# Grouped-query attention stage: two of TensorE's output units cut differently around its waits, one VectorE add moved ahead of a reciprocal, and the halves of the output-weight split exchanged between VectorE and GpSimd

## The chip, the cores and the metric

One core of one Trainium2 chip. The metric is device time in microseconds (us) of one execution; the kernel before took 3282.12 us, the median of 3 runs (3276.79 to 3284.53).

## What is computed

A two-layer gated transformer block with 16 x 128 rows of width 1024. Each layer adds a gated cross attention and a gated feed-forward part to the residual. The change lies in the third of these four parts, the grouped-query attention:

```python
q = (query @ Wq).reshape(b, t, h, d)          # h = 32 heads, d = 128
k = (key @ Wk).reshape(b, t, kv_h, d)         # kv_h = 8
v = (value @ Wv).reshape(b, t, kv_h, d)
q = apply_rope(q); k = apply_rope(k)
logits = MAX_ATTN_VAL * jnp.tanh(q.k * ATTN_MULT / MAX_ATTN_VAL)
logits = jnp.where(m, logits, -1e+30)
weights = jax.nn.softmax(logits, axis=-1)
attn = jnp.einsum('bkgtT,bTkd->btkgd', weights, v).reshape(b, t, h * d)
x = x + jnp.tanh(g_xattn[1]) * (attn @ Wo)
```

## The kernel before

The function `gqa_stage` runs 32 steps: 4 groups of 4 batches, and in each group the 8 key/value heads. A step n projects four query heads, rotates them, makes scores and probabilities for the 4 batches, sums and weights the values, normalises, and multiplies by that head's slice of `Wo` into the residual. Every engine has its own program, a list written out by hand, and semaphores tie them together. Each product in single precision is made of three matmuls (a high part times a high part, and the two mixed terms), so every operand is split into a rounded `hi`, made by ScalarE (`round_hi`, L1710), and a rest `lo`, made by GpSimd or VectorE (`subtract_hi`, L1569).

- **TensorE**: `attend(n)` and then `project(n + 1)`. `attend` runs `scores` (L1916, 3 matmuls), `values` (2 matmuls of row sums at L1925, 3 at L1931) and, between them, the output units of the step before: `out(u)` is unit u of 8 (batch u // 2, half u % 2), 12 matmuls at L1949, in four quarters of 3 matmuls, one a query head. `project` is 96 matmuls at L1893, 24 for each of the 4 query heads. That is 224 matmuls of 128x512 in a step.
- `scores(n, 0)` waits for all four rotated heads (`rot_lo`). Unit u waits for the add of unit u - 2, since both use one of two banks; units 0, 2, 4, 6 also wait for `at_lo` of their batch, and the four quarters of unit 0 wait for the four quarters of the split output weight. `values(n, b)` waits for `prob_lo` of b and for the reciprocal of b - 1 (`rsum_done`), since there is one bank for the row sums.
- **VectorE**: `rotate(n, i)` is three instructions (L1810 to L1812) that read a projected head from PSUM; it waits until GpSimd has added the head before (`rot_done`). `mask_probs` (L1844) multiplies by the mask, `normalise` is a reciprocal of 512 columns (L1850) and a product (L1853), `add(u)` is the add of an output unit into the residual (L1830), and `wo_split_dve` makes the `lo` of a quarter of the output weight (L1569).
- **GpSimd**: `rotated(n, i)` adds the two rotated parts (L1650), waits for ScalarE's rounding and subtracts (L1569). After heads 0 and 1 it makes the `lo` of an output-weight quarter (`wo_split`). Earlier in the step it makes the `lo` of the probabilities, of the attention output (`at`) and of the four quarters of the next `Wq` slice (`wq_split`); in the last step of a group these four stand behind the `lo` of the new activations.
- **ScalarE**: tanh and exp of the scores, the rounding of everything, in the order of `body_act`; the four quarters of the output weight are rounded one after the other, right behind rotated head 0.

In the last step the output weight lies in the buffer of `Wq` (`wo_last`), and the 8 output units run behind the last `values`, with the next stage's work between them.

Of the kernel before, what the change touches and what calls it, by code (L numbers as in the profile page):

```python
# [30 lines left out]
FIRST = 1  # L31
# [1416 lines left out]
def gqa_stage(nc, banks, kept_tiles, x_in, xnT, k_in, v_in, gate, Wq, Wo, x_out):  # L1448
# [8 lines left out]
    G = NH // NKV  # L1457
# [10 lines left out]
    def sem(name):  # L1468
        return nc.alloc_semaphore(name="g_" + name)
# [3 lines left out]
    def split(n, shape):  # L1473
        lo, hi = sb(n + "_lo", shape, F32R), sb(n + "_hi", shape, F32R)
        return {"lo": lo, "hi": hi, "raw": sb(n + "_raw", shape, over=n + "_lo")}
# [8 lines left out]
    wo, at = split("wo", [P, G, DM]), split("at", [P, G, BANK])  # L1484
# [3 lines left out]
    wo_last = {t: wq[t][:, :, :].rearrange("p (h a) n -> p h (a n)", h=G) for t in ("raw", "hi", "lo")}  # L1488
# [10 lines left out]
    wo_lo, wo_lo_dve, xn_lo, wq_lo = sem("wo_lo"), sem("wo_lo_dve"), sem("xn_lo"), sem("wq_lo")  # L1499
# [52 lines left out]
    def part(name, i, piece):  # L1552

        if name == "xn":
            c = (2 * i + piece) * SEQ
            return lambda t: t[:, :, c:c + SEQ]
        n = (KT if name == "wq" else G) // 4
        m = (2 * i + piece) * n
        return lambda t: t[:, m:m + n, :]

    def bcols(b):
        return slice(b * SEQ, (b + 1) * SEQ)

    def heads(t):
        return t.rearrange("p (h t) -> p h t", h=G)

    def subtract_hi(engine, buf, view):

        return engine.tensor_tensor(view(buf["lo"]), view(buf["raw"]), view(buf["hi"]).bitcast(F32), ALU.subtract)  # L1569

    sp, pool, act, dve, pe = nc.sync, nc.gpsimd, nc.scalar, nc.vector, nc.tensor
# [61 lines left out]
    def xn_split(g, i):  # L1633
        for m in range(2):
            pool.wait_ge(xn_hi, FIRST + g * 4 + 2 * i + m + 1)
            subtract_hi(nc.gpsimd, xn, part("xn", i, m)).then_inc(xn_lo, 1)

    def wq_split(n, m):
        pool.wait_ge(wq_hi, FIRST + n * 4 + m + 1)
        subtract_hi(nc.gpsimd, wq, part("wq", m // 2, m % 2)).then_inc(wq_lo, 1)  # L1640

    def wo_split(n, m, buf):
        pool.wait_ge(wo_hi, FIRST + n * 4 + m + 1)
        subtract_hi(nc.gpsimd, buf, part("wo", m // 2, m % 2)).then_inc(wo_lo, 1)

    def rotated(n, i):

        pool.wait_ge(rot_mul, FIRST + n * NR + i + 1)
        dst = q["raw"][:, i, :]
        nc.gpsimd.tensor_tensor(dst, dst, rot_b[:, :], ALU.add).then_inc(rot_done, 1)  # L1650
        pool.wait_ge(rot_hi, FIRST + n * NR + i + 1)
        subtract_hi(nc.gpsimd, q, lambda t: t[:, i, :]).then_inc(rot_lo, 1)
# [12 lines left out]
    def body_pool(z):  # L1665
        n = z.n

        def prob_split(b):
            pool.wait_ge(prob_hi, FIRST + n * NB + b + 1)
            subtract_hi(nc.gpsimd, prob[b % 2], lambda t: t[:, :]).then_inc(prob_lo, 1)  # L1670

        def attn_split(b):
            pool.wait_ge(at_hi, FIRST + n * NB + b + 1)
            subtract_hi(nc.gpsimd, at, lambda t: t[:, :, bcols(b)]).then_inc(at_lo, 1)

        early = not z.last and not z.group_end
        prob_split(0)
        prob_split(1)
        attn_split(0)
        prob_split(2)  # L1680
        if early:
            wq_split(n + 1, 0)
            wq_split(n + 1, 1)
        if z.group_end:
            xn_split(z.g + 1, 0)
        attn_split(1)
        prob_split(3)
        if z.group_end:
            xn_split(z.g + 1, 1)
        if early:  # L1690
            wq_split(n + 1, 2)
            wq_split(n + 1, 3)
        attn_split(2)
        if z.group_end:
            for m in range(4):
                wq_split(n + 1, m)
        if z.last:
            for m in range(2):
                wo_split(n, m, wo_last)
        attn_split(3)  # L1700
        if not z.last:
            for i in range(NR):
                rotated(n + 1, i)
                if i < 2:
                    wo_split(n, i, wo)


    A = nc.scalar.activation
# [79 lines left out]
    def wo_split_dve(n, m, buf):  # L1788
        dve.wait_ge(wo_hi, FIRST + n * 4 + m + 1)
        subtract_hi(V, buf, part("wo", m // 2, m % 2)).then_inc(wo_lo_dve, 1)  # L1790
# [42 lines left out]
    def body_dve(z):  # L1833
        n = z.n

        def add(*units):
            if not z.first:
                for u in units:
                    add_output(n - 1, u)

        def mask_probs(b):
            e = prob[b % 2]["raw"][:, :]
            dve.wait_ge(exp_done, FIRST + n * NB + b + 1)
            V.tensor_tensor(heads(e), heads(e), keep[:, :].rearrange("p (o t) -> p o t", o=1)  # L1844
                            .to_broadcast([P, G, SEQ]), ALU.mult).then_inc(masked, 1)

        def normalise(b):
            dve.wait_ge(sum_done, FIRST + n * NB + b + 1)
            dve.wait_ge(attn_done, FIRST + n * NB + b)
            V.reciprocal(rsum[:, :], p_sum[:, :]).then_inc(rsum_done, 1)  # L1850
            dve.wait_ge(rsum_done, FIRST + n * NB + b + 1)
            dve.wait_ge(pv_done, FIRST + n * NB + b + 1)
            V.tensor_tensor(at["raw"][:, :, bcols(b)], heads(p_pv[b % 2][:, :]), heads(rsum[:, :]), ALU.mult)\  # L1853
                .then_inc(attn_done, 1)

        if not z.first:

            dve.wait_ge(res_in, 64 * z.res_group + 64)
        add(0)
        mask_probs(0)  # L1860
        add(1)
        mask_probs(1)
        add(2)
        normalise(0)
        mask_probs(2)
        add(3)
        normalise(1)
        add(4)
        mask_probs(3)
        add(5)  # L1870
        normalise(2)
        if z.last:
            wo_split_dve(n, 2, wo_last)
        add(6, 7)
        normalise(3)
        if z.last:
            wo_split_dve(n, 3, wo_last)
        if not z.last:
            for i in range(NR):
                rotate(n + 1, i)  # L1880
                if 1 <= i < 3:
                    wo_split_dve(n, i + 1, wo)


    M, T = nc.tensor.matmul, nc.tensor.transpose
# [22 lines left out]
    def scores(n, b):  # L1908
        if b == 0:

            pe.wait_ge(rot_lo, FIRST + (n + 1) * NR)
            pe.wait_ge(k_land, 16 * n + 16)

        pe.wait_ge(tanh_done, FIRST + n * NB + max(b - 1, 0))
        for t, (p, r) in enumerate(SPLIT):
            mm = M(heads(p_s[b % 2][:, :]), k[p][:, bcols(b)], q[r][:, :, bcols(b)],  # L1916
                   start=(t == 0), stop=(t == 2))
        mm.then_inc(s_done, 1)
# [15 lines left out]
    def output(n, u, w, heads_=range(G)):  # L1934

        b, half_ = u // 2, u % 2
        if heads_[0] == 0:
            if half_ == 0:
                pe.wait_ge(at_lo, FIRST + n * NB + b + 1)

            pe.wait_ge(y_added, FIRST + n * NU + max(u - 1, 0))
        for h in heads_:
            if u == 0:
                if h < 2:
                    pe.wait_ge(wo_lo, FIRST + n * 2 + h + 1)
                else:
                    pe.wait_ge(wo_lo_dve, FIRST + n * 2 + h - 1)
            for t, (p, r) in enumerate(SPLIT):
                mm = M(p_y[u % 2][:, :], at[p][:, h, bcols(b)], w[r][:, h, half_ * BANK:(half_ + 1) * BANK],  # L1949
                       start=(h == 0 and t == 0), stop=(h == G - 1 and t == 2))  # L1950
        if heads_[-1] == G - 1:
            mm.then_inc(y_done, 1)

    def attend(n, first=False):
        def out(u, heads_=range(G)):
            if not first:
                output(n - 1, u, wo, heads_)

        out(0)
        out(1)  # L1960
        scores(n, 0)
        scores(n, 1)
        out(2)
        scores(n, 2)
        values(n, 0)
        out(3)
        out(4, range(0, 2))
        scores(n, 3)
        values(n, 1)
        out(4, range(2, G))  # L1970
        out(5)
        out(6, range(0, 1))
        values(n, 2)
        out(6, range(1, G))
        out(7)
        values(n, 3)

# [706 lines left out]
```

## Time and profile before

| | us |
|---|---|
| median of 3 runs | 3282.12 |
| lowest, highest | 3276.79, 3284.53 |
| the profiled execution's own time | 3288.88 |
| its span, from first to last instruction | 3287.1 |

Over the span TensorE's matmuls are busy 94%, VectorE 64%, GpSimd 56%, ScalarE 38%. The grouped-query stage takes from about 1280 us to 3063 us of the span, more than half of it. Engine shares are averages over stages with different limits; what bounds a step is read from the order of time inside one step, which repeats almost unchanged.

### The profile page before, as it was taken

The numbers are of one execution on the slowest core, as the hardware profiler recorded it, in microseconds if no ns is written. First come the engines' busy times: TensorE is split into PE (matmuls) and PEld (weight loads), VectorE is DVE, ScalarE is ACT, GpSimd is POOL, SyncE is SP. The second block draws the span as 40 slices with busy tenths as digits, with TensorE's granted clock in tenths as the row PEclk, the third lists the DMA queues.
The fourth block names the chain that finished last, engine by engine and source line by source line (L and its number), as shares of the span: only waits on it lengthen the run. The fifth ranks groups of instructions, "written<-read, shape, count | busy, mean of one in ns | idle before, by whom it ended". The sixth has DMA issues, their size and how long they took to land. (4 is left out here: it accounts for less than half of the span.)

```text
span 3287.1 us, 41110 instructions
## 1 busy us (share of the span) xinstructions
PE 3080.6 (94%) x14547; PEld 2474.0 (75%) x14547; DVE 2093.1 (64%) x2607; ACT 1234.8 (38%) x1898; POOL 1851.3 (56%) x1244
## 2 busy tenths in 40 slices
PE   7999679999999996899999999999999999998799
PEld 6888558788787775677777777777778787777577
DVE  3332357777777753767666767767777677676575
ACT  3111155555555541333333433433333434333222
POOL 4232354454454443667676767676767776764343
PEclk9999889999999997999999999999999999999799
DMA  7343501101111113222233222332222332323221
GB/s 200 107 131 109 180 26 39 65 33 65 53 45 65 52 54 114 102 90 102 89 128 141 102 95 96 121 147 96 96 96 101 129 134 96 111 90 134 84 71 52
DMA packets 171260, 315.53 MB, mean 96 GB/s; under 512 B 10328, under 2 KB 86488, under 8 KB 171144
## 3 DMA queue, kind: packets, MB, share of 16 engines
q1 hardware_dynamic: 171144, 314.04, 27.3%
q8 instruction: 66, 1.08, 0.1%
q14 instruction: 50, 0.41, 0.0%
HBM read 246.90 MB, written 67.11 MB: 96 GB/s over the span
## 5 line engine op out<-in xcount | busy, mean ns | idle before, releaser
L1850 DVE RECIPROCAL g_rsum<-pair 128x512 f32<-128x512 f32 x128 | 429.0, 3351 | 57.1 <-PE pair L1925 57.1
L1893 PE MATMUL pair<-g_xn_hi,g_wq_hi 128*128 128x512 f32 x1024 | 403.9, 394 | 19.1 <-POOL g_wq_lo L1569 14.0
L1893 PE MATMUL pair<-g_xn_lo,g_wq_hi 128*128 128x512 f32 x1024 | 402.5, 393 | 0.0
L1893 PE MATMUL pair<-g_xn_hi,g_wq_lo 128*128 128x512 f32 x1024 | 402.2, 393 | 0.0
L1949 PE MATMUL pair<-g_wo_hi,g_at_hi 128*128 128x512 f32 x992 | 389.6, 393 | 2.4 <-DVE g_res L1830 0.2
L1949 PE MATMUL pair<-g_wo_lo,g_at_hi 128*128 128x512 f32 x992 | 386.2, 389 | 0.0
L1949 PE MATMUL pair<-g_wo_hi,g_at_lo 128*128 128x512 f32 x992 | 386.1, 389 | 0.0
L1569 POOL TENSOR_TENSOR g_wq_lo<-g_wq_raw,g_wq_hi 128x1024 fp32r<-128x1024 f32 x130 | 310.9, 2415 | 0.0
L1569 POOL TENSOR_TENSOR g_at_lo<-g_at_raw,g_at_hi 128x512 fp32r<-128x512 f32 x128 | 180.1, 1407 | 217.6 <-ACT g_at_hi L1710 217.6
L1710 ACT ACTIVATE g_q_hi<-g_q_raw 128x512 fp32r<-128x512 f32 x128 | 81.0, 633 | 535.6 <-POOL g_q_raw L1650 535.6
L1810 DVE TENSOR_TENSOR g_q_raw<-pair,t_cos_q 128x512 f32<-128x512 f32 x128 | 88.5, 692 | 296.2 <-PE pair L1893 256.5
L1650 POOL TENSOR_TENSOR g_q_raw<-g_q_raw,g_rot_b 128x512 f32<-128x512 f32 x128 | 226.0, 1765 | 86.0 <-DVE g_rot_b L1812 86.0
L669 POOL TENSOR_TENSOR a_qs<-a_qs,a_qrec 128x512 f32<-128x512 f32 x128 | 133.9, 1048 | 201.2 <-DVE a_qrec L915 200.3
L1569 POOL TENSOR_TENSOR g_prob_lo<-g_prob_raw,g_prob_hi 128x512 fp32r<-128x512 f32 x128 | 166.6, 1311 | 138.1 <-ACT g_prob_hi L1710 138.1
L1893 PEld LDWEIGHTS pair<-g_xn_hi,g_wq_hi 128*128 128x128 f32 x1024 | 195.0, 190 | 62.9 <-POOL g_wq_lo L1569 16.7
L1844 DVE TENSOR_TENSOR g_prob_raw<-g_prob_raw,t_keep 128x512 f32<-128x512 f32 x128 | 132.5, 1035 | 166.7 <-ACT g_prob_raw L1741 166.7
L1949 PEld LDWEIGHTS pair<-g_wo_hi,g_at_hi 128*128 128x128 f32 x992 | 186.1, 188 | 53.4 <-DVE g_res L1830 14.9
L1893 PEld LDWEIGHTS pair<-g_xn_lo,g_wq_hi 128*128 128x128 f32 x1024 | 195.1, 191 | 40.7
L1893 PEld LDWEIGHTS pair<-g_xn_hi,g_wq_lo 128*128 128x128 f32 x1024 | 194.6, 190 | 40.9
L1569 POOL TENSOR_TENSOR g_q_lo<-g_q_raw,g_q_hi 128x512 fp32r<-128x512 f32 x128 | 165.0, 1289 | 95.1 <-ACT g_q_hi L1710 95.1
L1949 PEld LDWEIGHTS pair<-g_wo_hi,g_at_lo 128*128 128x128 f32 x992 | 186.2, 188 | 39.1
L1949 PEld LDWEIGHTS pair<-g_wo_lo,g_at_hi 128*128 128x128 f32 x992 | 186.3, 188 | 37.9
(251 smaller groups left out, 7333.3 us busy)
## 6 DMA issues: line engine op xcount, KB each, us to landing
g_wq_raw<-in_L_Wq SPq DMA_DIRECT2D x64, 1024.0 KB, 7.3
g_wo_raw<-in_L_Wo SPq DMA_DIRECT2D x62, 1024.0 KB, 6.3
values_split<-c_v SPq DMA_DIRECT2D x64, 256.0 KB, 2.8
keys_split<-c_k SPq DMA_DIRECT2D x32, 512.0 KB, 2.7
g_k<-keys_split SPq DMA_DIRECT2D x32, 512.0 KB, 3.2
g_v<-values_split SPq DMA_DIRECT2D x32, 512.0 KB, 7.7
c_cx_raw<-in_ctxT SPq DMA_DIRECT2D x16, 512.0 KB, 7.4
a_x<-in_x SPq DMA_DIRECT2D x16, 512.0 KB, 4.5
```

The costliest lines, as they stand in the source:

```text
L669: TT(t, t, spread(qrec[r % 2][:, :], DH), ALU.mult).then_inc(qnorm, 1)
L1569: return engine.tensor_tensor(view(buf["lo"]), view(buf["raw"]), view(buf["hi"]).bitcast(F32), ALU.subtract)
L1650: nc.gpsimd.tensor_tensor(dst, dst, rot_b[:, :], ALU.add).then_inc(rot_done, 1)
L1710: return A(view(buf["hi"]), view(buf["raw"]), ACT.Copy)
L1810: V.tensor_tensor(by_batch(a), by_batch(src[:, :]), w(cos, 0, P), ALU.mult)
L1844: V.tensor_tensor(heads(e), heads(e), keep[:, :].rearrange("p (o t) -> p o t", o=1) .to_broadcast([P, G, SEQ]), ALU.mult).then_inc(masked, 1)
L1850: V.reciprocal(rsum[:, :], p_sum[:, :]).then_inc(rsum_done, 1)
L1893: mm = M(bank[:, :], w[a][:, i, cols], x[b][:, i, :], start=(i == 0 and t == 0), stop=(i == KT - 1 and t == 2))
L1949: mm = M(p_y[u % 2][:, :], at[p][:, h, bcols(b)], w[r][:, h, half_ * BANK:(half_ + 1) * BANK], start=(h == 0 and t == 0), stop=(h == G - 1 ...
```

## The change

Three edits in `gqa_stage`, with the same instructions in all; only their order on an engine, and who splits which quarter, differ.

1. TensorE (`attend`): the first quarter of unit 2 goes ahead of the two first scores, the first half of unit 3 ahead of `scores(2)`, the second half of unit 4 ahead of `scores(3)`, the second quarter of unit 6 ahead of `values(2)`.
2. VectorE (`body_dve`): `add(4)` moves from behind the second `normalise` to ahead of it, right behind `add(3)`.
3. Output weight: VectorE now splits quarters 0 and 1, behind its rotations 0 and 1 (before: 2 and 3, behind 1 and 2), and GpSimd quarters 2 and 3, behind its rotated heads 0 and 1 as before (before: 0 and 1). The semaphores that unit 0 waits for are exchanged to match.

```diff
@@ body_pool
         if z.last:
-            for m in range(2):
+            for m in range(2, 4):
                 wo_split(n, m, wo_last)
         attn_split(3)
         if not z.last:
             for i in range(NR):
                 rotated(n + 1, i)
                 if i < 2:
-                    wo_split(n, i, wo)
+                    wo_split(n, i + 2, wo)
@@ body_dve
         mask_probs(2)
-        add(3)
+        add(3, 4)
         normalise(1)
-        add(4)
         mask_probs(3)
         add(5)
         normalise(2)
         if z.last:
-            wo_split_dve(n, 2, wo_last)
+            wo_split_dve(n, 0, wo_last)
         add(6, 7)
         normalise(3)
         if z.last:
-            wo_split_dve(n, 3, wo_last)
+            wo_split_dve(n, 1, wo_last)
         if not z.last:
             for i in range(NR):
                 rotate(n + 1, i)
-                if 1 <= i < 3:
-                    wo_split_dve(n, i + 1, wo)
+                if i < 2:
+                    wo_split_dve(n, i, wo)
@@ output
                 if h < 2:
-                    pe.wait_ge(wo_lo, FIRST + n * 2 + h + 1)
+                    pe.wait_ge(wo_lo_dve, FIRST + n * 2 + h + 1)
                 else:
-                    pe.wait_ge(wo_lo_dve, FIRST + n * 2 + h - 1)
+                    pe.wait_ge(wo_lo, FIRST + n * 2 + h - 1)
@@ attend
         out(1)
+        out(2, range(0, 1))
         scores(n, 0)
         scores(n, 1)
-        out(2)
+        out(2, range(1, G))
+        out(3, range(0, 2))
         scores(n, 2)
         values(n, 0)
-        out(3)
-        out(4, range(0, 2))
+        out(3, range(2, G))
+        out(4)
         scores(n, 3)
         values(n, 1)
-        out(4, range(2, G))
         out(5)
-        out(6, range(0, 1))
+        out(6, range(0, 2))
         values(n, 2)
-        out(6, range(1, G))
+        out(6, range(2, G))
         out(7)
         values(n, 3)
```

How the instructions stand on VectorE behind the rotations of one step, as a piece of the difference (- before, + changed): L1810 to L1812 are one rotation, L1569 is the split of an output-weight quarter.

```order
 L1811 TENSOR_TENSOR g_rot_b<-pair,t_sin_q 64x512
 L1812 TENSOR_TENSOR g_rot_b<-pair,t_sin_q 64x512
-L1810 TENSOR_TENSOR g_q_raw<-pair,t_cos_q 128x512
-L1811 TENSOR_TENSOR g_rot_b<-pair,t_sin_q 64x512
-L1812 TENSOR_TENSOR g_rot_b<-pair,t_sin_q 64x512
 L1569 TENSOR_TENSOR g_wo_lo<-g_wo_raw,g_wo_hi 128x1024
 L1810 TENSOR_TENSOR g_q_raw<-pair,t_cos_q 128x512
```

The first of the two splits now stands behind rotation 0, and rotation 1 behind the split; the second stands behind rotation 1, and between rotations 2 and 3 there is none.

VectorE from the second-to-last mask to the third reciprocal, in the kernel before:

```order
L1844 TENSOR_TENSOR g_prob_raw<-g_prob_raw,t_keep 128x512
L1830 SCALAR_TENSOR_TENSOR g_res<-pair,g_tg,g_res 128x512
L1850 RECIPROCAL g_rsum<-pair 128x512
L1853 TENSOR_TENSOR g_at_raw<-pair,g_rsum 128x4x128
L1830 SCALAR_TENSOR_TENSOR g_res<-pair,g_tg,g_res 128x512
L1844 TENSOR_TENSOR g_prob_raw<-g_prob_raw,t_keep 128x512
L1830 SCALAR_TENSOR_TENSOR g_res<-pair,g_tg,g_res 128x512
L1850 RECIPROCAL g_rsum<-pair 128x512
```

and in the changed one:

```order
L1844 TENSOR_TENSOR g_prob_raw<-g_prob_raw,t_keep 128x512
L1830 SCALAR_TENSOR_TENSOR g_res<-pair,g_tg,g_res 128x512 x2
L1850 RECIPROCAL g_rsum<-pair 128x512
L1853 TENSOR_TENSOR g_at_raw<-pair,g_rsum 128x4x128
L1844 TENSOR_TENSOR g_prob_raw<-g_prob_raw,t_keep 128x512
L1830 SCALAR_TENSOR_TENSOR g_res<-pair,g_tg,g_res 128x512
L1850 RECIPROCAL g_rsum<-pair 128x512
```

The add of unit 4 joins that of unit 3, and the last mask (the second L1844) follows the second product (L1853) directly.

## Rows read from the trace of the kernel before

**Rows 1.** Windows, an ordinary and a group's last step: start:end length, busy per engine, PEclk, DMA, GB/s.

```profile
1549.10:1602.38 53.28, 51.68 (x225) 41.81 (x224) 37.97 (x35) 19.86 (x28) 37.02 (x23) 1.00 0.27 98
1655.66:1713.69 58.03, 51.87 (x226) 41.62 (x224) 42.03 (x37) 24.15 (x33) 41.95 (x26) 0.99 0.47 155
```

**Rows 2.** Timeline, TensorE, one ordinary step: start us, us, instruction, [idle before <-releaser].

```profile
1517.60 0.39 PE L1949 MATMUL pair<-g_wo_hi,g_at_hi 128*128 128x512 f32 x1
...
1524.29 0.49 PE L1916 MATMUL pair<-g_q_hi,g_k 128*128 128x512 f32 x1 [1.09 <-POOL g_q_lo L1569]
...
1529.80 0.50 PE L1925 MATMUL pair<-g_prob_hi,g_ones_r 128*128 128x512 f32 x1 [0.47 <-POOL g_prob_lo L1569]
...
1535.83 0.39 PE L1925 MATMUL pair<-g_prob_hi,g_ones_r 128*128 128x512 f32 x1
...
1541.28 0.50 PE L1949 MATMUL pair<-g_wo_hi,g_at_hi 128*128 128x512 f32 x1
...
1547.99 0.39 PE L1925 MATMUL pair<-g_prob_hi,g_ones_r 128*128 128x512 f32 x1
...
1549.12 0.39 PE L1893 MATMUL pair<-g_xn_hi,g_wq_hi 128*128 128x512 f32 x1
```

**Rows 3.** Timeline, VectorE, rotations 1 to 3 of the same step.

```profile
1506.92 0.69 DVE L1810 TENSOR_TENSOR g_q_raw<-pair,t_cos_q 128x512 f32<-128x512 f32 x1 [3.19 <-PE pair L1893]
...
1509.04 1.54 DVE L1569 TENSOR_TENSOR g_wo_lo<-g_wo_raw,g_wo_hi 128x1024 fp32r<-128x1024 f32 x1
...
1514.48 2.73 DVE L1569 TENSOR_TENSOR g_wo_lo<-g_wo_raw,g_wo_hi 128x1024 fp32r<-128x1024 f32 x1
1518.59 0.69 DVE L1810 TENSOR_TENSOR g_q_raw<-pair,t_cos_q 128x512 f32<-128x512 f32 x1 [1.38 <-POOL g_q_raw L1650]
```

**Rows 4.** Timeline, ScalarE's four output-weight roundings and GpSimd, the same stretch.

```profile
1505.66 3.89 ACT L1710 ACTIVATE g_wo_hi<-g_wo_raw 128x1024 fp32r<-128x1024 f32 x4
...
1507.10 2.41 POOL L1569 TENSOR_TENSOR g_wo_lo<-g_wo_raw,g_wo_hi 128x1024 fp32r<-128x1024 f32 x1
1509.46 2.27 POOL L1650 TENSOR_TENSOR g_q_raw<-g_q_raw,g_rot_b 128x512 f32<-128x512 f32 x1
...
1513.73 2.41 POOL L1569 TENSOR_TENSOR g_wo_lo<-g_wo_raw,g_wo_hi 128x1024 fp32r<-128x1024 f32 x1
1516.07 2.29 POOL L1650 TENSOR_TENSOR g_q_raw<-g_q_raw,g_rot_b 128x512 f32<-128x512 f32 x1
...
1520.77 1.29 POOL L1650 TENSOR_TENSOR g_q_raw<-g_q_raw,g_rot_b 128x512 f32<-128x512 f32 x1 [0.37 <-DVE g_rot_b L1812]
```

**Rows 5.** Timeline, VectorE, from the second add to the third reciprocal.

```profile
1527.27 0.74 DVE L1830 SCALAR_TENSOR_TENSOR g_res<-pair,g_tg,g_res 128x512 f32<-128x512 f32 x1
...
1530.66 3.36 DVE L1850 RECIPROCAL g_rsum<-pair 128x512 f32<-128x512 f32 x1 [1.21 <-PE pair L1925]
...
1534.66 0.68 DVE L1844 TENSOR_TENSOR g_prob_raw<-g_prob_raw,t_keep 128x512 f32<-128x512 f32 x1
1535.26 0.74 DVE L1830 SCALAR_TENSOR_TENSOR g_res<-pair,g_tg,g_res 128x512 f32<-128x512 f32 x1
1536.48 3.36 DVE L1850 RECIPROCAL g_rsum<-pair 128x512 f32<-128x512 f32 x1 [0.48 <-PE pair L1925]
...
1540.48 0.74 DVE L1830 SCALAR_TENSOR_TENSOR g_res<-pair,g_tg,g_res 128x512 f32<-128x512 f32 x1
1541.14 2.16 DVE L1844 TENSOR_TENSOR g_prob_raw<-g_prob_raw,t_keep 128x512 f32<-128x512 f32 x1
...
1543.88 3.34 DVE L1850 RECIPROCAL g_rsum<-pair 128x512 f32<-128x512 f32 x1
```

**Rows 6.** Timeline, GpSimd, the first two quarters of the next query weight.

```profile
1537.99 4.76 POOL L1569 TENSOR_TENSOR g_wq_lo<-g_wq_raw,g_wq_hi 128x1024 fp32r<-128x1024 f32 x2
```

**Rows 7.** Timeline, TensorE, first projection behind the last step of a group.

```profile
1713.69 0.79 PE L1893 MATMUL pair<-g_xn_hi,g_wq_hi 128*128 128x512 f32 x1 [4.61 <-POOL g_wq_lo L1569]
```

**Rows 8.** Timeline, TensorE, fourth quarter of unit 0 behind the last step.

```profile
3018.11 0.50 PE L1949 MATMUL pair<-g_wq_hi,g_at_hi 128*128 128x512 f32 x1 [1.35 <-DVE g_wq_lo L1569]
```

## Prediction

> **What bounds the kernel now.** First the windows of the grouped-query stage: an ordinary step takes 53.28 us, the last step of a group 58.03 us [rows 1]. Then TensorE's timeline through one ordinary step. Five matmuls without a wait take 1549.12 - 1547.99 = 1.13 us, so 0.227 us each, and the 224 of a step 50.8 us. TensorE is the bound, and only 53.28 - 50.8 = 2.4 to 2.5 us a step are waits. There are three [rows 2], and the first matmuls behind each run about 0.1 us late:
> - ahead of the first scores: units 0 and 1 (24 matmuls, 5.45) run from 1517.60 to 1523.05, the scores start at 1524.29, so 1.24. They wait for the last rotated head.
> - ahead of the first values (1529.80): of the 5.51 us since the scores' start, 21 matmuls and the late start take 4.87, so 0.64; GpSimd's `prob_lo` was late.
> - ahead of unit 6 (1541.28): 23 matmuls (5.22) since 1535.83, so 0.23 at its bank, which the add of unit 4 frees at 1540.48 + 0.74 = 1541.22 [rows 5].
>
> Two more views show what these waits hang on. VectorE's and GpSimd's timelines of the rotations: VectorE's split of a quarter, asked for at 1509.04, ends at 1510.58, which is 1.07 behind the end of GpSimd's split (1509.51); GpSimd's add, begun at 1509.46, ends at 1511.73, 1.15 behind VectorE's. The second pair (1514.48 and 1516.07) ends 1.07 behind 1516.14 and 1.15 behind 1517.21 in the same way, where an unhindered add takes 1.29 [rows 3, 4]. So these two engines exclude each other here, instruction by instruction. The mask at 1541.14 (2.16 instead of 0.68) ends at 1543.30, 0.55 behind the end (1542.75) of the second query-weight quarter [rows 5, 6]. The rotations and the reciprocals read PSUM and keep their lengths.
>
> **The change, edit by edit.** No instruction is added or taken away, and no DMA moves, so everything is a shift of waits.
>
> *Exchange of the output-weight quarters.* ScalarE's four roundings run 1505.66 to 1509.55, about 0.95 apart [rows 4]. GpSimd's first split took quarter 0, ready early, and began at 1507.10. It now needs quarter 2, ready at about 1508.60, begins at 1508.68 and ends at 1511.09. VectorE splits quarter 0 from 1507.14 (GpSimd's subtraction ends there) to about 1508.2, so rotation 1 slips from 1506.92 to 1508.1 and ends at 1510.2 (2.12 long [rows 3]). It asks for quarter 1 at 1510.1, waits for GpSimd, and ends at 1511.09 + 1.07 = 1512.16. GpSimd's add of head 1 then ends at 1512.16 + 1.15 = 1513.31, where it was 1511.73. Its second split comes 2.00 later as before (1511.73 to 1513.73 [rows 4]), 1515.31 to 1517.72. Now the gain: no VectorE split stands there, so the add of head 2 takes 1.29 and ends at 1517.65 + 1.29 = 1518.94, against 1518.36. Rotation 3 waits for exactly this add [rows 3], and the scores for rotation 3. So the first scores start 0.58 later: **+0.58 us**. Bounds: 0 if the add of head 2 is not held at all, and 0.58 + 1.0 if one more collision of the kind in rows 3 and 4 falls in. I take 0.58, since each link has its row.
>
> *First quarter of unit 2 ahead of the scores.* 27 matmuls end at 1517.60 + 6.13 = 1523.73, before the scores can start (1524.87). It costs nothing and fills 0.68 of that wait.
>
> *From the first scores to the last values*, counted from the scores' start as 0. Before, the last values started at 1547.99 - 1524.29 = 23.70. Now:
> - scores 0 and 1 and three quarters of unit 2 end at 1.46 + 2.04 = 3.50. Unit 3 needs the add of unit 1, which ends at 1527.27 + 0.74, so 3.72 [rows 5]: a new wait until 3.78. Six matmuls and a late start: 5.25. Scores 2: 5.93.
> - the first values start at 5.93 without a wait (`prob_lo` is there at 5.51). The second come 26 matmuls later, 11.83. The first reciprocal starts 0.65 behind the values (1535.83 to 1536.48 [rows 2, 5]), at 6.58; before it was 6.37.
> - VectorE: mask 4.00 behind the reciprocal, then 0.60 (mask) and twice 0.66 (adds): second reciprocal at 12.50, its sums at 12.48. The moved add just fills the idle 0.48 [rows 5]. The last mask is asked for 4.00 later, at 16.50.
> - GpSimd's second query-weight quarter starts 9.71 behind the first reciprocal (1540.37 - 1530.66 [rows 5, 6]) and ends 12.09 behind it: 16.29 to 18.67. The mask is late by 0.21 and waits for all of it: end at 18.67 + 0.55 = 19.22. The add of unit 5 ends at 19.88, the third reciprocal runs 19.80 to 23.14; before it started at 19.59.
> - TensorE reaches unit 7 at 11.83 + 34 x 0.227 = 19.55 and waits for that add until 19.94, then has 12 matmuls, and meets the last values at 22.77. These wait for the third reciprocal: 23.20, and with the late start the next projection begins at 24.43. Before: 24.83.
>
> So the two old waits (0.64 and 0.23, with their late starts) are gone and three others come, because VectorE's third reciprocal does not come earlier. **-0.40 us.**
>
> The length of a mask that waits is taken from the row: 0.55 behind GpSimd's end [rows 5, 6]. The Trainium skill, "SBUF — State Buffer", section "Who interferes with whom", says that the second instruction blocks fully until the first has finished. Read strictly that puts the whole 0.68 behind, and VectorE's chain 0.13 later; the sum would be +0.31 a step and 3293 us. The row decides for 0.55, since it shows this very pair.
>
> A bound of the -0.40 below: -1.43, the next section's first rival; above, +0.2, if VectorE's whole chain is 0.6 later.
>
> *Sum.* An ordinary step gains +0.58 - 0.40 = +0.18 us. There are 31 intervals between first projections; the first has no output units, 3 end a group. 27 x 0.18 = 4.9 us. In a group's last step the projection waits 4.76 us for GpSimd, whose chain through the probabilities sets it [rows 7]: there only the delays count, 0.58 + 0.21 = 0.8, three times, 2.4 us. In the last step quarter 3 of unit 0 waited for VectorE's split [rows 8]; now quarter 1 does, so 6 more matmuls (1.4 us) stand behind it, but VectorE's first split no longer waits for the third rounding (about 1.9 us, two roundings): I take 0, with 1.5 either way. Sum **+7.3 us**. The profiled execution, 3288.88 us, becomes 3296.2; it lies 6.8 above the median, so the median goes from 3282.12 to **3289.4 us**. About 0.2%, 6.6 us, is what a measurement here can tell from no change.
>
> **The rivals.**
> - *The mask gets ahead* (faster). Everything at that place hangs on 0.21 us: is the last mask asked for before the second query-weight quarter begins, it takes 0.68. The reciprocal can start at 17.8, ends at 21.1, unit 7 and the last values do not wait, the next projection starts at 22.27 + 1.13 = 23.40, so 1.43 earlier than before. With the exchange's 0.58: -0.85 a step, 27 x -0.85 + 2.4 = -21 us, **3262 us**. For it: only 0.21 us decide. Against: all the durations repeat within 0.03 us, and the margin is a difference of chains that start from the same reciprocal. 0.12. The Trainium skill, "SBUF — State Buffer", section "Who interferes with whom", has this as its rule: of a VectorE instruction with two SBUF inputs and a GpSimd one that reads SBUF, whoever issues first gets the shared port pair.
> - *The exchange is free* (faster). If GpSimd's add of head 2 ends no later than before, the -0.40 stays: 27 x -0.40 + 3 x 0.2 = -10 us, **3272 us**. For it: the stall of 1.0 on that add does go. Against: the 1.58 lost at the third rounding is larger. 0.14.
> - *The delay is larger* (slower). A longer idle ahead of the first projection of a group (4.76 grows to 5.4) or one more collision in the rotations: up to 0.3 a step more, +15 us, **3297 us**. It decides if the scores come more than 0.8 late. 0.14.
> - *Nothing moves.* If the new waits just take the place of the old ones and the exchange evens out, 3282 us. 0.06.
>
> **How the numbers follow.** The forecast case has 0.54, and its own range is 3285 to 3294 (0.15 us a step). Of it 0.30 lies above +6.6 us and 0.24 within. With the rivals: faster 0.12 + 0.14 = 0.26; slower 0.30 + 0.14 = 0.44; the same 0.24 + 0.06 = 0.30. The range of 8 in 10 leaves out the first rival and the far end of the third: 3270 to 3299.
>
> **What the changed profile would show.** An ordinary step of 53.4 to 53.5 us. GpSimd's add of head 1 stretched to about 2.3 us and that of head 2 at 1.3. The idle time ahead of the scores still near 1.1 us, now 27 matmuls behind the projection. No wait at the first values; short waits at unit 3, unit 7 and the last values, the last released by the third reciprocal. The last mask about 2.7 us long. A last mask of 0.7 us, or an ordinary step under 53.1, would make the prediction wrong; so would an add of head 2 that ends less than 0.3 later behind the start of the projection.

## Result, and the profile after

| | before, us | changed, us |
|---|---|---|
| median (5 runs each) | 3280.46 | 3297.67 |
| lowest to highest | 3276.79 to 3284.53 | 3293.07 to 3299.62 |
| profiled execution, own time | 3288.88 | 3297.86 |
| its span | 3287.1 | 3296.1 |

The ratio is 1.0049, with a 95% interval of 1.0037 to 1.0060: the change makes the kernel slower by 12 to 20 us. The forecast was +7.3 us (3289.4 us, range 3270 to 3299), with a chance of 0.44 for a slower kernel.

The windows of the changed kernel, as in [rows 1]: first projection of the stage to the last one, from there to the end, one ordinary step, one last step of a group. The columns are those of [rows 1].

```profile
1279.41:2967.61 1688.20, 1607.23 (x6849) 1286.45 (x6849) 1144.69 (x1042) 622.43 (x877) 1135.32 (x690) 0.99 0.30 108
2967.61:3296.10 328.49, 289.84 (x1329) 225.41 (x1327) 201.81 (x306) 92.89 (x168) 132.52 (x96) 0.90 0.23 87
1495.72:1549.41 53.69, 51.92 (x225) 41.74 (x224) 37.36 (x36) 19.85 (x29) 36.03 (x23) 1.00 0.27 98
1656.76:1715.62 58.86, 52.06 (x225) 41.53 (x223) 41.99 (x38) 24.17 (x34) 41.41 (x26) 0.99 0.46 161
```

The same two stretches of the kernel before, first profile:

```profile
1280.67:2955.46 1674.79, 1598.22 (x6848) 1288.74 (x6849) 1162.07 (x1042) 622.31 (x877) 1164.52 (x690) 0.99 0.30 109
2955.46:3287.10 331.64, 292.56 (x1329) 226.64 (x1327) 202.42 (x305) 92.89 (x167) 134.82 (x96) 0.90 0.23 87
```

The loss lies between the first and the last projection: 1688.20 - 1674.79 = 13.4 us. Most ordinary steps are now 53.56 to 53.70 us and were 53.15 to 53.30, so 0.40 more (the first one of a group is some 3 us longer in both kernels, and grows by 0.3 to 0.4); the three last steps of a group are 58.87 to 58.97 and were 57.99 to 58.04, 0.92 more. 27 x 0.40 + 3 x 0.92 = 13.6. VectorE and GpSimd are busy for less time than before (1144.69 and 1135.32 us against 1162.07 and 1164.52), and the stretch is longer all the same.

TensorE's timeline in the ordinary step, which answers to [rows 2]: the scores, unit 3, the first and second values, unit 7, the last values, the next projection.

```profile
1524.79 0.49 PE L1915 MATMUL pair<-g_q_hi,g_k 128*128 128x512 f32 x1 [1.01 <-POOL g_q_lo L1569]
...
1528.57 0.50 PE L1948 MATMUL pair<-g_wo_hi,g_at_hi 128*128 128x512 f32 x1
...
1530.75 0.39 PE L1924 MATMUL pair<-g_prob_hi,g_ones_r 128*128 128x512 f32 x1
...
1536.64 0.39 PE L1924 MATMUL pair<-g_prob_hi,g_ones_r 128*128 128x512 f32 x1
...
1544.84 0.50 PE L1948 MATMUL pair<-g_wo_hi,g_at_hi 128*128 128x512 f32 x1 [0.33 <-DVE g_res L1830]
...
1548.19 0.47 PE L1924 MATMUL pair<-g_prob_hi,g_ones_r 128*128 128x512 f32 x1 [0.34 <-DVE g_rsum L1850]
...
1549.41 0.39 PE L1892 MATMUL pair<-g_xn_hi,g_wq_hi 128*128 128x512 f32 x1
```

The wait at the first values is gone (no bracket at 1530.75; 0.47 before), and in its place stand three: at unit 3 (1528.57, a first matmul of 0.50 instead of 0.39), at unit 7 (1544.84) and at the last values (1548.19), the last two released by an add and by the reciprocal of VectorE. From the scores to the next projection it is 1549.41 - 1524.79 = 24.62 us, where [rows 2] gives 24.83.

GpSimd in the same step, which answers to [rows 4]:

```profile
1508.60 2.41 POOL L1569 TENSOR_TENSOR g_wo_lo<-g_wo_raw,g_wo_hi 128x1024 fp32r<-128x1024 f32 x1 [1.55 <-ACT g_wo_hi L1710]
1510.96 2.27 POOL L1650 TENSOR_TENSOR g_q_raw<-g_q_raw,g_rot_b 128x512 f32<-128x512 f32 x1
...
1515.22 2.39 POOL L1569 TENSOR_TENSOR g_wo_lo<-g_wo_raw,g_wo_hi 128x1024 fp32r<-128x1024 f32 x1
1517.56 1.30 POOL L1650 TENSOR_TENSOR g_q_raw<-g_q_raw,g_rot_b 128x512 f32<-128x512 f32 x1
```

The projection began at 1495.72 here and at 1495.84 in [rows 2]. The first split waits 1.55 us for ScalarE's third rounding, the add of head 1 is stalled (2.27), the add of head 2 is not (1.30). It ends at 1518.86, 23.14 behind the projection's start; before it was 22.52. The scores start 29.07 behind it, before 28.45.

VectorE, which answers to [rows 5]:

```profile
1531.49 3.36 DVE L1850 RECIPROCAL g_rsum<-pair 128x512 f32<-128x512 f32 x1 [1.71 <-PE pair L1924]
1534.88 0.69 DVE L1853 TENSOR_TENSOR g_at_raw<-pair,g_rsum 128x512 f32<-128x512 f32 x1
1535.49 0.68 DVE L1844 TENSOR_TENSOR g_prob_raw<-g_prob_raw,t_keep 128x512 f32<-128x512 f32 x1
1536.09 1.41 DVE L1830 SCALAR_TENSOR_TENSOR g_res<-pair,g_tg,g_res 128x512 f32<-128x512 f32 x2
1537.41 3.35 DVE L1850 RECIPROCAL g_rsum<-pair 128x512 f32<-128x512 f32 x1
1540.79 0.69 DVE L1853 TENSOR_TENSOR g_at_raw<-pair,g_rsum 128x512 f32<-128x512 f32 x1
1541.40 2.72 DVE L1844 TENSOR_TENSOR g_prob_raw<-g_prob_raw,t_keep 128x512 f32<-128x512 f32 x1
1544.04 0.74 DVE L1830 SCALAR_TENSOR_TENSOR g_res<-pair,g_tg,g_res 128x512 f32<-128x512 f32 x1
1544.70 3.34 DVE L1850 RECIPROCAL g_rsum<-pair 128x512 f32<-128x512 f32 x1
```

The moved add has filled the idle 0.48 ahead of the second reciprocal. The last mask is asked for 0.24 us earlier behind the scores than before (16.61 against 16.85) and takes 0.56 longer, 2.72 instead of 2.16, because GpSimd's quarter ends no earlier: 18.78 behind the scores (1543.57), before 18.46. The third reciprocal starts 19.91 behind the scores, before 19.59.

### The profile page after: what moved, and what is told of

Same layout as the page of the kernel before. It is cut to its first block and busy times, and to the rows that moved or that the text cites. A ratio compares the mean times of both kernels' runs of the same rounds, so it can differ in the third digit from the quotient of the medians.

```text
span 3296.1 us, 41110 instructions
## 1 busy us (share of the span) xinstructions
PE 3084.4 (94%) x14547; PEld 2468.6 (75%) x14547; DVE 2076.7 (63%) x2607; ACT 1235.3 (37%) x1898; POOL 1819.9 (55%) x1244
## 5 line engine op out<-in xcount | busy, mean ns | idle before, releaser
L1569 POOL TENSOR_TENSOR g_wq_lo<-g_wq_raw,g_wq_hi 128x1024 fp32r<-128x1024 f32 x130 | 309.5, 2402 | 1.6 <-ACT g_wq_hi L1710 1.6
L1569 POOL TENSOR_TENSOR g_at_lo<-g_at_raw,g_at_hi 128x512 fp32r<-128x512 f32 x128 | 178.9, 1398 | 224.1 <-ACT g_at_hi L1710 224.1
L1844 DVE TENSOR_TENSOR g_prob_raw<-g_prob_raw,t_keep 128x512 f32<-128x512 f32 x128 | 150.1, 1172 | 167.5 <-ACT g_prob_raw L1741 167.5
L1569 POOL TENSOR_TENSOR g_prob_lo<-g_prob_raw,g_prob_hi 128x512 fp32r<-128x512 f32 x128 | 167.1, 1315 | 138.0 <-ACT g_prob_hi L1710 138.0
L1810 DVE TENSOR_TENSOR g_q_raw<-pair,t_cos_q 128x512 f32<-128x512 f32 x128 | 88.6, 692 | 238.2 <-POOL g_q_raw L1650 149.2
L1650 POOL TENSOR_TENSOR g_q_raw<-g_q_raw,g_rot_b 128x512 f32<-128x512 f32 x128 | 195.6, 1528 | 72.0 <-DVE g_rot_b L1812 72.0
L1569 POOL TENSOR_TENSOR g_q_lo<-g_q_raw,g_q_hi 128x512 fp32r<-128x512 f32 x128 | 164.8, 1287 | 95.1 <-ACT g_q_hi L1710 95.1
```

Of the source, the lines that this page charges most:

```text
L1810: V.tensor_tensor(by_batch(a), by_batch(src[:, :]), w(cos, 0, P), ALU.mult)
```

## The experiments

Every kernel was timed beside the kernel before on the same chip (medians of 3280 to 3284 us).

### 1. Without the exchange

The whole change, minus its edits to `body_pool`, `wo_split_dve` and the waits of unit 0:

```diff
-                    wo_split(n, i + 2, wo)
+                    wo_split(n, i, wo)
-                if i < 2:
-                    wo_split_dve(n, i, wo)
+                if 1 <= i < 3:
+                    wo_split_dve(n, i + 1, wo)
```

> The change without its exchange of the output-weight quarters: only TensorE's new unit order and VectorE's moved add. The theory: the exchange alone makes the first scores 0.58 to 0.59 us later, and the rest gives back 0.2 us from the scores to the next projection (24.62 us in the changed kernel against 24.83 before). So an ordinary step takes about 53.0 us (before 53.2, changed 53.6), the first scores start 28.45 us behind the projection as before, and the time is some 5 us below the kernel before, 3272 to 3278 us. The rival, that the exchange is free and the slowdown comes from the new waits at units 3 and 7 and the last values: an ordinary step stays at 53.6 us and the time at 3295 us or more.

Measured: 3275.89 us against 3284.05, ratio 0.9978 (0.9969 to 0.9987). An ordinary step is 52.96 us, and the scores start 28.34 us behind the projection in most steps, as in the kernel before (28.33) and not as in the changed one (28.95). The theory held, the rival fell: TensorE's and VectorE's edits together gain 0.2 us a step, and the exchange turns that into a loss of 0.4. A group's last step, though, is 0.3 us longer than in the kernel before (58.32 against 58.03).

### 2. The exchange alone

The edits above the other way round, on the kernel before.

> The exchange alone, with TensorE's and VectorE's order of before. The theory: GpSimd's first output-weight split waits for ScalarE's third rounding and ends 1.5 to 1.6 us later, the add of head 1 ends 1.6 later, that of head 2 only 0.58, and every ordinary step is 0.6 us longer, 53.8 us; the time rises by 27 x 0.6 + 3 x 0.6 = 18 us, less some 2 us in the last step: 3295 to 3300 us. The rival, that the exchange is free: 53.2 us a step and no change.

Measured: 3302.98 us, ratio 1.0058 (1.0044 to 1.0072). An ordinary step is 53.77 to 53.82 us, 0.6 more, as expected, and a group's last step 58.63 (0.6 more); the rival fell. The time lies above the 3295 to 3300 expected. The 2 us that the last step was to give back did not come: the third of its output units starts 70.69 us behind the last projection, before 69.14. GpSimd in one of these steps, with the first split released by ScalarE and one stalled add, just as in the changed kernel:

```profile
1509.15 2.41 POOL L1569 TENSOR_TENSOR g_wo_lo<-g_wo_raw,g_wo_hi 128x1024 fp32r<-128x1024 f32 x1 [1.55 <-ACT g_wo_hi L1710]
1511.52 2.27 POOL L1650 TENSOR_TENSOR g_q_raw<-g_q_raw,g_rot_b 128x512 f32<-128x512 f32 x1
...
1518.12 1.30 POOL L1650 TENSOR_TENSOR g_q_raw<-g_q_raw,g_rot_b 128x512 f32<-128x512 f32 x1
```

The two parts add: -0.2 and +0.6 are the +0.4 of the change, and in a group's last step +0.3 and +0.6 are its +0.9.

### 3. The exchange with VectorE's splits in their old places

```diff
-                if i < 2:
-                    wo_split_dve(n, i, wo)
+                if 1 <= i < 3:
+                    wo_split_dve(n, i - 1, wo)
```

> The exchange alone, but VectorE's two splits stay where they stood, behind rotations 1 and 2; only which quarter each engine takes is exchanged. The theory of two engines that exclude each other: both adds on GpSimd are stalled by about 1.0 us, since a VectorE split stands ahead of each; the add of head 2 ends some 1.5 us later than before, the scores too, and an ordinary step takes 54.7 to 54.9 us, the time 3322 to 3330 us. The rival, that only the place behind the rotations costs and not the later quarter: 53.2 us a step, 3281 us.

Measured: 3336.90 us, ratio 1.0160 (1.0146 to 1.0174), an ordinary step of 54.80 us. This time both adds are stalled:

```profile
1514.45 2.40 POOL L1569 TENSOR_TENSOR g_wo_lo<-g_wo_raw,g_wo_hi 128x1024 fp32r<-128x1024 f32 x1 [1.55 <-ACT g_wo_hi L1710]
1516.80 2.28 POOL L1650 TENSOR_TENSOR g_q_raw<-g_q_raw,g_rot_b 128x512 f32<-128x512 f32 x1
...
1523.43 2.27 POOL L1650 TENSOR_TENSOR g_q_raw<-g_q_raw,g_rot_b 128x512 f32<-128x512 f32 x1
```

So the exchange has a loss, the later quarter (about 1.6 us a step), and a gain, the place of the second split (1.0); the rival that only the place counts fell. No run rounds quarter 2 first on ScalarE, so that its third rounding causes the loss rests on the wait in brackets (1.55) and on this comparison. The step is as expected, the time lies 7 us above the range given (3322 to 3330): behind the last projection the profile has 334 us, as in experiment 2, where the kernel before has 329 to 332.

### 4. The kernel before, once more

> The kernel before, once more, for a second profile: the first one's execution lay 8 us above the median of the others. If that is chance outside the grouped-query stage, the first projections are again 53.2 to 53.3 us apart, 1675 us from the first to the last, and what differs lies ahead of 1280 us or behind 3063 us; if the steps themselves vary from execution to execution, they differ by 0.1 to 0.3 us each.

Measured: 3283.02 us, ratio 0.9995 (0.9986 to 1.0005). Its profile:

```profile
1280.29:2954.40 1674.11, 1599.28 (x6848) 1289.36 (x6849) 1161.79 (x1042) 622.24 (x877) 1164.30 (x690) 0.98 0.30 109
2954.40:3283.00 328.60, 289.95 (x1329) 224.96 (x1327) 202.79 (x305) 92.89 (x167) 134.52 (x96) 0.91 0.23 88
```

The steps repeat (1674.11 against 1674.79); 3.0 of the first profile's excess lie behind the last projection. That the first spans differ by 9.0 us and not by the 13.4 of the stage comes from this stretch (3.1) and from 1.3 us ahead of the stage. Places where the program is the same vary by as much: the stage begins at 1276.5 to 1280.7 us in the profiles of this document.

### 5 and 6. TensorE's order alone, VectorE's add alone

> TensorE's new unit order alone, VectorE's add of unit 4 still behind the second normalise, no exchange. The theory: unit 6 now waits for that add as long as before or longer, and the third reciprocal starts where it did, behind the add and the stalled last mask, so the early quarters of units 2 and 3 bring nothing: an ordinary step takes 53.4 us (before 53.2) and the time rises by 3 to 8 us. The rival, that the unit order is what gains and the moved add is only along: 53.0 us, as in the kernel without the exchange.

> VectorE's add of unit 4 ahead of the second normalise, with TensorE's order of before, in which unit 4 ends behind the second values. The theory: the second reciprocal now waits for unit 4, which ends 11 matmuls behind the start of the second values, so it starts about 1.8 us later, and the third reciprocal and the last values with it: an ordinary step of 54.0 us or a little more, the time 23 to 28 us up. The rival, that the add only fills idle time: 53.2 us or less.

Measured: 3295.09 us, ratio 1.0036 (1.0023 to 1.0050), a step of 53.50 us, for TensorE's order; 3306.47 us, ratio 1.0076 (1.0062 to 1.0090), a step of 53.87, for the add. Each alone is slower, and the two together gain 0.2 us (experiment 1). With the units alone the wait at unit 6 grows from 0.23 to 1.59 us, since it comes earlier and its add does not; that cost 0.3 us a step where 0.2 was expected, and the time rose by 12 us where 3 to 8 were expected. With the add alone the time rose by 24 us, within the 23 to 28 expected, and the second reciprocal waits for unit 4:

```profile
1535.62 0.75 DVE L1830 SCALAR_TENSOR_TENSOR g_res<-pair,g_tg,g_res 128x512 f32<-128x512 f32 x1
1538.89 0.75 DVE L1830 SCALAR_TENSOR_TENSOR g_res<-pair,g_tg,g_res 128x512 f32<-128x512 f32 x1 [2.52 <-PE pair L1948]
1539.56 3.35 DVE L1850 RECIPROCAL g_rsum<-pair 128x512 f32<-128x512 f32 x1
...
1543.55 0.68 DVE L1844 TENSOR_TENSOR g_prob_raw<-g_prob_raw,t_keep 128x512 f32<-128x512 f32 x1
```

The reciprocal starts 2.7 us later, 14.9 behind the scores instead of 12.19, and not 1.8: the expectation had left out the add itself, which takes most of the difference (1538.89 to 1539.56). Only 0.7 of it reach the step, because the last mask is now so late that GpSimd's quarter is over, and takes 0.68 us instead of 2.16. That was not in the expectation either; the two errors partly cancel, so that the time was right is in part luck. It is also the first run that shows the mask free.

### 7 and 8. The query-weight quarter moved away from the last mask

The next theory was that in the changed kernel the stalled mask alone sets the third reciprocal, and that the last values. GpSimd's second quarter moves, first on the kernel of experiment 1, then on the whole change:

```diff
         prob_split(2)
         if early:
             wq_split(n + 1, 0)
-            wq_split(n + 1, 1)
...
         prob_split(3)
...
         if early:
+            wq_split(n + 1, 1)
             wq_split(n + 1, 2)
             wq_split(n + 1, 3)
```

> The change without its exchange, and GpSimd's second query-weight quarter moved from ahead of the attention output of batch 1 to behind the probabilities of batch 3, so that no GpSimd instruction is under way when VectorE asks for its last mask. The theory (the last mask, stalled behind that quarter, pins the third reciprocal, which pins the last values): the last mask takes 0.7 us instead of 2.7, the third reciprocal starts 1.9 to 2.0 us earlier behind the scores and no longer holds the last values, the waits at unit 7 and at the last values are gone, an ordinary step takes 51.7 to 51.8 us, and the time falls by 27 x 1.2 = 33 us below the kernel without the exchange: 3240 to 3248 us. The rival, that the last values wait for something else, or that a later quarter makes the projection late: 52.9 us or more.

> The whole change, exchange included, with the same move of GpSimd's second query-weight quarter. The theory: the exchange's 0.6 us and the stalled mask's 1.2 us are separate terms and add, so an ordinary step takes 52.3 to 52.4 us and the time is 17 to 20 us above the kernel of the run before, 3260 to 3268 us. The rival, that with a freed third reciprocal the exchange no longer costs, or costs more: 51.8 us, or 53 us and more.

Measured: 3241.42 us, ratio 0.9880 (0.9865 to 0.9896), and 3260.55 us, ratio 0.9936 (0.9923 to 0.9950); ordinary steps of 51.74 and 52.34 us. VectorE and GpSimd of the first:

```profile
1526.32 3.35 DVE L1850 RECIPROCAL g_rsum<-pair 128x512 f32<-128x512 f32 x1
...
1530.31 0.68 DVE L1844 TENSOR_TENSOR g_prob_raw<-g_prob_raw,t_keep 128x512 f32<-128x512 f32 x1
1530.91 0.75 DVE L1830 SCALAR_TENSOR_TENSOR g_res<-pair,g_tg,g_res 128x512 f32<-128x512 f32 x1
1531.57 3.35 DVE L1850 RECIPROCAL g_rsum<-pair 128x512 f32<-128x512 f32 x1
```

```profile
1527.73 2.41 POOL L1569 TENSOR_TENSOR g_wq_lo<-g_wq_raw,g_wq_hi 128x1024 fp32r<-128x1024 f32 x1
1531.14 1.30 POOL L1569 TENSOR_TENSOR g_at_lo<-g_at_raw,g_at_hi 128x512 fp32r<-128x512 f32 x1 [1.00 <-ACT g_at_hi L1710]
```

GpSimd is idle for 1.00 us ahead of 1531.14, the mask falls into that gap and takes 0.68 us, and the third reciprocal starts 5.25 us behind the second instead of 7.29. TensorE waits neither at unit 7 nor at the last values. The last steps of a group, which the edit does not touch, keep their length (58.32). The step is 1.22 us shorter (52.96 to 51.74) and, with the exchange in, 1.26 (53.60 to 52.34): the exchange's 0.6 stands by itself beside it. Both times lie in their ranges, and both rivals fell.

### 9 and 10. Two steps further

On experiment 7, first `add(0, 1)` ahead of the first mask; then, in a group's last step, the attention output of batch 2 behind the four query-weight quarters:

```diff
-        add(0)
-        mask_probs(0)
-        add(1)
+        add(0, 1)
+        mask_probs(0)
         mask_probs(1)
```

```diff
-        attn_split(2)
+        if not z.group_end:
+            attn_split(2)
         if z.group_end:
             for m in range(4):
                 wq_split(n + 1, m)
+            attn_split(2)
```

> On top of the kernel without the exchange and with the late query-weight quarter: VectorE adds unit 1 right behind unit 0, ahead of its first mask. The theory: unit 3 then waits for nothing (0.23 us and a late start of 0.1 in each step go), and the first mask, which waits for exp, is not later, since the add fits into VectorE's idle time ahead of it: 0.3 us less a step, 51.4 to 51.5 us, and 3229 to 3236 us. The rival, that the first values then wait for the probabilities instead: 51.7 us and no gain.

> On top of the last: in the last step of a group GpSimd splits the four query-weight quarters ahead of the attention output of batch 2, which stands 1.27 us long ahead of them and is needed only by unit 4 of the next step. The theory, that in such a step GpSimd's chain alone holds the projection: 58.3 us becomes 57.0 us three times, 4 us less in all. The rival, that the first quarter waits for ScalarE's rounding, which comes behind its own attention output: a gain of less than 0.5 us each.

Measured: 3235.40 us, ratio 0.9851 (0.9838 to 0.9864), steps of 51.40 us, 0.34 less, with no wait left at unit 3, as expected; and 3229.64 us, ratio 0.9840 (0.9827 to 0.9853), with last steps of a group of 56.74 to 56.81 us, 1.2 less than the 57.98 to 58.04 of experiment 9. The intervals of these two overlap, so the second step rests on its profile, and there on the group ends alone: from the first to the last projection it is 2.9 us shorter and not 3.6, as the first step of the stage, which the edit does not touch, is 1.0 us longer (52.89 against 51.86). Both are faster than the kernel before and than the change; the last lies 54 us below the one and 68 below the other.

## Why the prediction was right, and where it was too small

The mechanism held link by link, and the size was half of what was measured: +7.3 us forecast, +13.4 in the stage, 12 to 20 in the runs. The time, 3297.67 us, is outside the forecast case's own range (3285 to 3294), and so is the step (53.6 us, not 53.4 to 53.5). It happens to be the figure of the rival with the larger delay (3297), but that rival's sign, scores more than 0.8 us late, did not show: they are 0.62 late.

- **The exchange, +0.58 us.** The scores start 29.07 behind the projection, before 28.45: 0.62 in the changed kernel, 0.6 alone (experiment 2). The 0.04 above the forecast are 1.1 us over 27 steps. The quarter's wait, the stalled add of head 1 and the free add of head 2 are where the working put them.
- **The first quarter of unit 2, nothing.** It fills part of the wait, as forecast: the scores start as late without the exchange as in the kernel before (experiment 1).
- **From the first scores to the next projection, -0.40 us.** This is the term that was mis-sized: it measured 24.62 - 24.83 = -0.21. Two links were each about 0.1 short. The first reciprocal starts 6.70 behind the scores, not 6.58: it came 0.74 behind the first values (1530.75 to 1531.49), where I had taken the 0.65 of the second values, and the values came 0.03 later. Everything on VectorE and GpSimd up to the third reciprocal hangs on it, and starts at 19.91 instead of 19.80. And the last values start 0.15 behind that reciprocal's end (1548.04 to 1548.19), not 0.06, a step taken from a wait for an add. Why these two steps differ from the rows that I took them from stays open.
- **The count.** 0.19 us on 27 ordinary steps is 5.1 us, and 0.12 on three group ends 0.4: with them the sum is 12.8, and 13.9 with the 1.1 of the exchange, where the stage measured 13.4.
- **The last step, nothing.** Its waits moved as forecast: quarter 1 of unit 0 now waits 4.1 us, quarter 3 waited 1.35, and the third output unit starts 69.22 us behind the last projection, before 69.14. From there to the end of these units the changed kernel takes 36.0 us at a mean granted clock of 0.81, the kernel before 38.9 at 0.74, in both of its profiles; these are means of pieces at 2.4 and at 1.2 GHz. So up to that end the last step gained 2.8 us, more than the 1.5 allowed for, in a stretch that the working did not treat. Behind it the program is the same and takes 223.2 us at 0.91 in the changed kernel, 223.6 at 0.90 and 220.6 at 0.92 in the two profiles of the kernel before. That the whole stretches of the second profile and of the changed kernel agree (328.60 and 328.49) is therefore chance.

```profile
3024.60:3063.52 38.92, 33.27 (x121) 25.02 (x119) 11.45 (x23) 11.34 (x19) 4.67 (x2) 0.74 0.11 45
3036.83:3072.86 36.03, 30.45 (x121) 23.27 (x119) 11.51 (x23) 10.72 (x19) 4.71 (x2) 0.81 0.10 40
```

- **The rival of the mask that gets ahead** did not happen: the second quarter begins at 1541.18, the mask is asked for at 1541.40, 0.22 later (forecast 0.21), and takes 2.72. Its price was right where the collision was taken away: it put the next projection 23.40 us behind the scores, and in experiments 7 and 8 it is at 23.4, against 24.83 in the kernel before; its time was 3262 us, and experiment 8, which has the exchange too, took 3260.55.
- **The waiting mask.** The Trainium skill ("SBUF — State Buffer", "Who interferes with whom") says that whoever issues first gets the shared port pair for the whole instruction and the other fully blocks. Read strictly, that is an estimate of 0.68 from the end of GpSimd's quarter to the end of the mask. The quarters begin at 1538.82 and take 4.75 for both in this profile, so they end at 1543.57; the mask ends at 1544.12, 0.55 behind. The row's value holds, and a full block is a little more than this pair shows.

```profile
1538.82 4.75 POOL L1569 TENSOR_TENSOR g_wq_lo<-g_wq_raw,g_wq_hi 128x1024 fp32r<-128x1024 f32 x2
```

## What to carry to other kernels

A wait that an edit removes is worth only what the next one behind it leaves: here two waits on TensorE went away (0.64 and 0.23 us), and a reciprocal that had not come earlier handed most of it back, so look for what pins that chain (here a 0.7 us mask stalled for 2 us behind another engine's work; taking that collision away was worth six times what the reordering gained). Edits that shift two engines' orders against each other must be timed together and apart: two of the three parts lose alone and gain as a pair, and the third costs the same 0.6 us a step on each of the three kernels that it was added to.

## What the runs showed that was not expected

- VectorE's delay can cure itself. In experiment 6 the second reciprocal was 2.7 us later and the step only 0.7 longer, since the mask behind it came out from under GpSimd's quarter (0.68 instead of 2.16 us).
- A kernel's end can differ by more than the edit in it. The stretch behind the last projection measured 325.5 to 334.3 us over all the profiles. Its second part, behind the last output unit of the stage, is the same program in all, and took 220.6 us at a granted clock of 0.92 in one profile of the kernel before and 226.0 at 0.89 in experiment 2. What sets that clock from run to run is not shown.
